# One block instead of two: the set-up of an attention and FFN kernel ordered among the first batch's work, with its staging laid over late buffers

## The reference

```
x = x + attention(layernorm(x), ctx, ctx)      # q = xn @ Wq.T + bq, k, v from ctx; q and k rotated by a phase per head
x = x + ffn(layernorm(x))
ffn: gf = sigmoid(MLP of the mean over the 1024 rows)
     out = x;  3 times: tf = sigmoid(gelu(gelu(gelu(out@w1)@w2)@w3)@w4)
                        out = out + (0.1 + range * (0.7*gf + 0.3*tf - 0.5) * 2) * twist(out)
```

## Time and profile before

| | us |
|---|---|
| median of 3 runs | 1504.09 |
| lowest and highest | 1503.36, 1508.3 |
| profiled execution, its own time | 1504.29 |
| its span, first to last instruction | 1502.2 |

### The profile page before, as it was taken

One profiled execution on the slowest core, in us unless ns is written; L12 is line 12 of the kernel. 1 busy time (PEld: TensorE's weight loads), 2 busy tenths in 40 slices (PEclk: granted clock), 3 DMA queues, 4 the chain that ended last, 5 costly groups with the idle time before them and its releaser, 6 DMA issues.

```text
span 1502.2 us, 29586 instructions
## 1 busy us (share of the span) xinstructions
PE 1322.3 (88%) x11288; PEld 930.1 (62%) x11288; DVE 1144.5 (76%) x2247; ACT 1058.3 (70%) x1949; POOL 643.8 (43%) x499
## 2 busy tenths in 40 slices
PE   6556789898999899999999899989999899989765
PEld 3333376666766586657766676658666676658553
DVE  3749538996599958996799759995898759983476
ACT  2635258876698769877797678877787768876565
POOL 0304114563255615563355516561455426561463
PEclk9866899999999999999999999999999999999986
DMA  8203400321124031312124122403132113301001
GB/s 271 85 11 70 110 2 18 65 57 50 51 57 75 1 106 34 60 39 65 43 57 75 32 75 44 78 12 96 26 64 54 50 57 57 71 1 43 1 15 43
DMA packets 156399, 83.36 MB, mean 55 GB/s; under 512 B 138978, under 2 KB 140770, under 8 KB 154211
## 3 DMA queue, kind: packets, MB, share of 16 engines
q1 hardware_dynamic: 156258, 81.47, 22.5%
HBM read 27.97 MB, written 19.92 MB: 32 GB/s over the span
## 4 chain that ended last, share of the span: by engine, by line
PE 54%; DVE 21%; ACT 9%; issue 6%; POOL 4%; DMA 1%; ACTq 0%; DVEq 0%
PE ps L283 20%; PE ps L241 9%; PE ps L298 8%; PE ps L196 7%; DVE prob L1666 2%; DVE mx L1658 2%; PE ps L318 2%; DVE pr L1688 2%; DVE z L1759 2%; PE ps L173 2%; POOL Y L2732 2%; DVE h L1738 2%; POOL h L2716 2%; DVE sm L1673 1%; PE ps L214 1%
## 5 line engine op out<-in xcount | busy, mean ns | idle before, releaser
L2716 POOL TENSOR_TENSOR h<-z,h 128x512 f16<-128x512 f32 x192 | 250.1, 1311 | 363.7 <-DVE h L1731 363.7
L283 PE MATMUL ps<-x2T,W 128*128 128x256 f16 x3072 | 356.6, 274 | 7.3 <-ACT Y L774 4.6
L283 PEld LDWEIGHTS ps<-x2T,W 128*128 128x128 f16 x3072 | 298.9, 98 | 53.6 <-issue 8.4
L298 PE MATMUL ps<-h,W 128*128 128x256 f16 x2304 | 283.6, 280 | 25.2 <-POOL h L2716 25.1
L298 PEld LDWEIGHTS ps<-h,W 128*128 128x128 f16 x2304 | 226.8, 100 | 74.5 <-issue 36.8
L2709 POOL TENSOR_TENSOR prob<-prob,rc 128x512 f32<-128x512 f32 x128 | 149.7, 1190 | 95.6 <-DVE rc L1682 95.5
L241 PE MATMUL ps<-WO,xoT 128*128 128x512 f16 x768 | 180.6, 386 | 4.4 <-DVE xoT L1693 4.4
L196 PE MATMUL ps<-xoT,WQ 128*128 128x512 f16 x768 | 175.2, 386 | 1.4 <-DVE xoT L1641 1.4
L787 ACT ACTIVATE z<-z,b_col 128x256 f32<-128x256 f32 x256 | 115.6, 499 | 33.1 <-DVE z L1759 32.8
L241 PEld LDWEIGHTS ps<-WO,xoT 128*128 128x128 f16 x768 | 75.9, 99 | 92.2 <-DVE xoT L1693 6.5
L196 PEld LDWEIGHTS ps<-xoT,WQ 128*128 128x128 f16 x768 | 76.0, 99 | 89.3 <-issue 5.9
(11 more groups left out here) (148 smaller groups left out, 2373.9 us busy)
## 6 DMA issues: line engine op xcount, KB each, us to landing
xin<-x SPq DMA_DIRECT2D x16, 1024.0 KB, 6.3
out<-ot SPq DMA_DIRECT2D x64, 256.0 KB, 3.4
kv_blocks<-kv SPq DMA_DIRECT2D x8, 384.0 KB, 3.8
kvb<-kv_blocks SPq DMA_DIRECT2D x8, 384.0 KB, 3.1
pT<-pr SPq DMA_TRANSPOSE x128, 3.2
ctx_s<-ctxT SPq DMA_DIRECT2D x4, 256.0 KB, 3.5
wv_s<-wvT SPq DMA_DIRECT2D x1, 1024.0 KB
wk_s<-wk SPq DMA_DIRECT2D x1, 1024.0 KB, 9.6
```

Source lines behind the costliest of these rows:

```text
L283: mm = e.matmul(ps[:, BANK_F + L, at * LBLK:(at + 1) * LBLK], w, v, start=(n == 0), stop=(n == 3 * C - 1))
L298: mm = e.matmul(ps[:, BANK_F + L, m * LBLK:(m + 1) * LBLK], w, v, start=(c + m + a == 0), stop=(c == C - 1 and m == C2 - 1 and a == 2))
L2716: e.tensor_tensor(h1[:, L, LO, pair(n)], z[:, L, pair(n)], h1[:, L, HI, pair(n)], ALU.subtract).then_inc(lg[L]["lo1"], 1)
```

## The change

There is now one block. The function `setup` is gone; its work is cut into pieces (`wq_turn`, `wk_turn`, `bias`, `kmul`, `vmul` on TensorE; `wq_hi`, `wk_out`, `k_hi`, `v_hi`, `w_hi` on ScalarE; `wq_lo`, `bias_out`, `k_lo`, `v_lo`, `w_lo`, `w_neg` and others on VectorE), and they stand in the lists of the batches, among the first steps of batch 0. Wq and x come first in the loads. K's low parts are all VectorE's. The four memsets of `kv` on VectorE come later. V uses three PSUM banks in turn and so waits for `v_lo` of three batches before. K and V of batch 0 go from `kv` to `kvb` directly, within SBUF; those of the others still go through DRAM, each with a semaphore of its own. The staging tiles are allocated ahead of x2T, pT, pr, Y, z and the FFN's other buffers and given free before them, so they share memory; the first steps that write there wait for the pieces that read the staging. The lists of the batches were written anew and differ from before by small moves; instructions and tiles of the batches are the same.

```diff
+            def vmul(bt):
+                if bt < 3:
+                    e.wait_ge(su["k_out"], bt + 2)
+                else:
+                    e.wait_ge(su["v_lo"], 2 * (bt - 3) + 2)
...
             def y(p, k, h, m):
...
+                    if u == 0:
+                        for n in range(1, B):
+                            e.wait_ge(kv_stored[n], 16)
+                        e.wait_ge(su["w_lo"], 6)
...
+            def k_lo(m):
+                for h in range(HPC):
+                    rows = slice(DK * h, DK * h + DK)
+                    e.wait_ge(su["k_hi"], HPC * m + h + 1)
+                    e.tensor_tensor(kpart(LO)[rows, :, m, h % 2], k32[rows, m], kpart(HI)[rows, :, m, h % 2],
+                                    ALU.subtract).then_inc(su["k_lo"], 1)
...
-            t1(0, 0, 0); t1(0, 0, 1); t1(0, 0, 2); t1(0, 0, 3)
+            wq_turn(0, 0); wq_turn(0, 1); wq_turn(0, 2); wq_turn(0, 3)
+            wk_turn(0, 0); wk_turn(0, 1); wk_turn(0, 2); wk_turn(0, 3)
+            bias(0)
+            kmul(0, 0); kmul(0, 1); kmul(0, 2); kmul(0, 3)
+            vmul(0, 0)
+            t1(0, 0, 0)
+            vmul(0, 1); vmul(0, 2); vmul(0, 3)
+            t1(0, 0, 1)
...
-            def kv(b):
+            def kv_load(b):
                 if b:
                     e.wait_ge(sg["s"], 8 * b)
                     e.wait_ge(sg["pv"], 4 * b)
-                e.dma_start(kvb[:].rearrange("p a n -> p (a n)"), kv_dram[b]).then_inc(sg["kv_loaded"], 16)
+                    e.wait_ge(kv_stored[b], 16)
+                    src = kv_dram[b]
+                else:
+                    e.wait_ge(su["v_hi"], 2)
+                    e.wait_ge(su["v_lo"], 2)
+                    e.wait_ge(su["k_lo"], HPC * C)
+                    src = kv[:, 0].rearrange("p a n -> p (a n)")
+                e.dma_start(kvb[:].rearrange("p a n -> p (a n)"), src).then_inc(sg["kv_loaded"], 16)
...
+            load("wq", wq_s[:], by_chunk(wq))
+            load_x(0)
+            load("wk", wk_s[:], by_chunk(wk))
...
+            load_x(1)
+            load("wo", wo_s[:], by_chunk(woT))
...
+            kv_load(0)
+            kv_store(0, 1); kv_store(0, 2); kv_store(0, 5); kv_store(0, 3); kv_store(0, 4); kv_store(0, 6); kv_store(0, 7)
```

More of the change, by code:

```diff
@@ L36 @@
 KV = KCOLS + PAIRS * DK
+ATT_PAD = 577
 def passes(parts_a, parts_b):
@@ L140, in program @@
             "alpha", "t_out", "out")}
+        su = {n: sem(n) for n in (
+            "consts", "zero_v", "zero_g", "angle", "sines", "rotation", "v_mul", "v_hi", "v_lo", "bias_mul", "bias_out", "bo_split",
+            "wk_mul", "wk_out", "k_mul", "k_out", "k_hi", "k_lo", "w_hi", "w_lo", "w_neg", "last_row", "wq_mul",
+            "wq_hi", "wq_lo", "scalars")}
+        loaded = {n: sem(f"in_{n}") for n in (
+            "phases", "turns", "ctx", "wv", "wk", "bqk", "wq", "wo", "bo", "w1", "w2", "w3", "last", "g1", "g2", "scal", "cols")}
         stored = [sem(f"stored{i}") for i in range(OUTS)]
@@ L896, in scalar_program @@
             yc(0, 0, 1, 2)
+            qh(1, 0, 0)
             act2(0, 0, 0, 0, 0)
-            qh(1, 0, 0)
+            xn1(1, 1, 0)
+            qh(1, 0, 1)
             act2(0, 0, 0, 0, 1)
@@ L1374, in scalar_program @@
             hi2(6, 0, 0, 0)
+            xn1(7, 1, 2)
             qh(7, 0, 2)
@@ new lines, in k_lo, with v_lo @@
+            @first
+            def k_lo(m):
+                for h in range(HPC):
+                    rows = slice(DK * h, DK * h + DK)
+                    e.wait_ge(su["k_hi"], HPC * m + h + 1)
+                    e.tensor_tensor(kpart(LO)[rows, :, m, h % 2], k32[rows, m], kpart(HI)[rows, :, m, h % 2],
+                                    ALU.subtract).then_inc(su["k_lo"], 1)
+            @first
+            def v_lo(bt):
+                for h in range(2):
+                    rows = slice(KEYS * h, KEYS * h + KEYS)
+                    src = ps[rows, BANK_V[bt % 3], 0:D2].rearrange("p (r n) -> p r n", r=PAIRS)
+                    e.wait_ge(su["v_hi"], 2 * bt + h + 1)
+                    e.tensor_tensor(vpart(LO)[rows, bt], src, vpart(HI)[rows, bt], ALU.subtract).then_inc(su["v_lo"], 1)
@@ new lines, in w_lo, with w_neg @@
+            @first
+            def w_lo(n):
+                e.wait_ge(su["w_hi"], n + 1)
+                dst, src = split_parts[n]
+                e.scalar_tensor_tensor(dst[:, LO], src[:], WSCALE, dst[:, HI], ALU.mult, ALU.subtract).then_inc(su["w_lo"], 1)
+            @first
+            def w_neg():
+                e.wait_ge(su["w_lo"], 2)
+                for p in (HI, LO):
+                    e.tensor_scalar(W1[:, p, C:C + 2], W1[:, p, 1:3], -1.0, None, ALU.mult).then_inc(su["w_neg"], 1)
@@ new lines, in sync_program @@
+            load("bqk", b_s[:, 1], bk)
+            load("wv", wv_s[:], by_chunk(wvT))
+            load("wv", bv_s[:], row(bv))
+            load_x(1)
+            load("wo", wo_s[:], by_chunk(woT))
+            load("bo", bo_s[:], row(bo).partition_broadcast(P))
+            load("last", last_s[:, 0:1], cw4)
+            load("last", last_s[:, 1:2], gw3)
+            for n, a in enumerate((arange, cb4, gb3)):
+                load("scal", scal_s[:, n:n + 1], row(a).partition_broadcast(P))
+            load("w1", w1_s[:], by_chunk(cw1))
```

1210 lines of the change are left out of this document (609 added, 601 removed).

## The result

| | before | after |
|---|---|---|
| time, median of 4 runs each (lowest to highest) | 1504.41 us (1503.36 to 1508.30) | 1465.75 us (1464.11 to 1466.76) |
| span of the profiled execution | 1502.2 us | 1464.2 us |
| first scores of batch 0 | 104.56 | 79.24 |
| from there to the first scores of batch 1 | 132.2 | 135.0 |
| six stretches, batch 1 to batch 7 | 995.2 | 983.9 |

In the profiled executions the first scores come 25.3 us earlier (forecast 22.4), the first stretch gives 2.8 back, and the rest, forecast as nothing, is 11.3 + 4.3 = 15.6 us shorter.

What follows compares the result with a forecast made beforehand. The prediction saw a serial set-up of small steps delaying batch 0's first scores to 104.56 us; scores 22.4 us earlier, less 0.5 in batch 0's softmax, took 1504.3 to 1482.4, said as 1482.5 us, range 1474.5 to 1491.5.

Steps and rivals of the forecast that it cites:

- Step 1: Set-up loads: Wq lands at 9 us, x block 0 at 12.3, Wo at 26.5, 6 us later than before.
- Rival A: Set-up: a stall on ScalarE or VectorE, as from Wo landing at 35, eats half the gain; 1493 us, chance 0.09.
- Steps 2 and 3: Set-up products: Wk at half clock, bias product done at 26.8 us; K 14.00 us plus 3 for a half-clock start.
- Bounds: Low: full clock for Wk and K (4.5 us), batches slightly shorter, 1475 us; high: late Wo, slower low parts, 1491.
- Step 4: VectorE in the set-up: K's 16 low parts at 0.68 us each, other weights' low parts, first xl1 at 57.4 us.
- Step 5: V pieces alternate with x's transposes on TensorE; the first Q product starts at 68.7 us, before at 90.03.
- Step 6: First Q product to scores: Q 10.4 us at full clock, V 7 2.45, transposes 0.65; scores at 82.2 us.
- Sum: Whole kernel: scores 22.4 us earlier, less 0.5, changed order in the batches taken as nothing; 1482.4, said as 1482.5 us.
- rival D: Batches: the new order gives besides, xn1(p,1,0) filling ScalarE's 1.2 us wait, 1 us or more each; 1474 us, chance 0.11.
- The cost I did charge, 0.5 us: Batch 0's softmax: v_hi(7) and v_lo(7) now stand inside it, 0.84 us, half in a hole, so 0.5.
- Rival B: Set-up: TensorE stays at half clock throughout, scores at 108.7 us, no gain; 1508 us, chance 0.03.
- Rival C: Batches: new order costs more than the start gives, l2 ahead of tile 2's scores on TensorE; 1517 us, chance 0.05.

Runs made afterwards that it cites:

- e11: Changed kernel with half of K's 16 low parts given back from VectorE to GpSimd; 1466.49 us.
- e2: Kernel before, its two blocks and layout kept, with every engine's list from batch 1 on in the changed kernel's order; 1491.12 us.
- e1: Changed kernel with every engine's list from batch 1 on in the order of before, set-up and batch 0 kept; 1479.22 us.
- e7: Changed kernel with only ScalarE's list from batch 1 on in the order of before; 1468.76 us.
- e14: Kernel before with only GpSimd's product mulg(p,1,0,2) put behind both am steps in batches 1 to 6; 1500.27 us.
- e8: Changed kernel with only TensorE's list from batch 1 on in the order of before; 1471.40 us.
- e6: Changed kernel with only VectorE's list from batch 1 on in the order of before; 1477.46 us.
- e10: Changed kernel with VectorE's xl2(b,0,0) put back behind the second pair of statistics in batches 2 to 6; 1466.18 us.
- e13: Changed kernel with GpSimd's product mulg(p,1,0,2) put ahead of both am steps in all eight batches; 1477.12 us.

## Why the prediction was wrong in size and right in kind

The sign, the mechanism of the start and the order of the terms held; the range did not. By its own steps:

- **Step 1 (loads)**: Wo landed at 24.8 instead of 26.5. Rival A's late load did not come, yet ScalarE waited 1.0 us for it, since it was through with xn at 23.8 instead of 28.
- **Steps 2 and 3 (Wq, Wk, K)**: too slow by 5 us at the end of the bias product (22.0 instead of 26.8), and K took 13.98 us instead of 17. VectorE reached wq_lo at 16.7 instead of 18.6. For the rest I had charged half clock for the pause; TensorE ran Wk's last 24 matmuls in 2.94 us and K at a full clock. This was the gain named in "Bounds", low. (The list of K's ends also gives the last piece 1 us more than the two ahead of it, for which no row stands.)
- **Step 4 (VectorE, which carries most)**: right. 16 low parts at 0.68 and G's at 1.22 + 0.42; the first low part of x at 51.1 instead of 57.4, since all began earlier. e11 confirms why 0.68 was the number to take: beside GpSimd the median is 1.53.
- **Step 5**: from there to Q, 14.6 us instead of 11.3. Here the clock did fall (0.72 and 0.64), and of the V pieces two took 3.03 and 3.67 us. The half clock I had put at K came at V. Q at 65.7, forecast 68.7.
- **Step 6**: right; 13.5 us from Q to scores, as forecast. First scores 79.24 instead of 82.2.
- **Sum, the failing step**: "The changed order in the batches I take as nothing." It gives 14.1 and 13.5 us in e2 and e1. It is rival D, mis-sized (0 in the sum, 8 us in the rival, about 13 measured) and under-weighted (0.11), and its reason was wrong: what I named for it, ScalarE's xn1(p,1,0), belongs to the list that e7 prices at 3.0 us for all its moves. The largest single move found is GpSimd's mulg(p,1,0,2): 6.4 us in e14. The view that would have led there was open: the row of c <- c in the kernel before, shown above, has instances of 293 and of 1242 ns, and GpSimd's product runs beside the long one (664.62 to 666.13 beside 665.03 to 666.27). I had used this very effect in step 4 and did not look for it in the batches.
- **The cost I did charge, 0.5 us** for v_hi(7) and v_lo(7) in batch 0's softmax: the first stretch was 2.8 us longer. The first stretch's length also moves between kernels with the same lists up to there (133.2 to 135.3 us), so at least 1 us of it is real and the rest is not settled.
- **Rival B** fell with K's full clock. One of its readings was off: before, the granted clock over 95 to 98 us is 1.00 already, so it was back within 5 us of the Q product's start at 90.03, and not only behind 8 us of it. **Rival C**: the scores of tile 2 came 1.3 us later in the stretch (554.38 - 542.05 = 12.33 instead of 11.02), but the product of the first probabilities 0.2 us earlier (615.76 - 542.05 = 73.71 instead of 644.61 - 570.67 = 73.94), so the delay is absorbed within the batch. e8, with TensorE's old list, takes 5.6 us more: that engine's moves gain and don't cost. TensorE in the changed kernel:

```profile
554.38 0.84 PE L301 MATMUL ps<-kvb,qT 64*128 64x128 f16 x24
...
615.76 0.84 PE L317 MATMUL ps<-pT,kvb 64*32 64x512 f16 x24
```


The start by itself was forecast at 21.9 us and measured at 26.0 (before to e1) and 25.4 (e2 to after): 3.5 to 4 us too little, and e1's 1479.2 lies inside the range. Step by step the errors went both ways (K 8 us earlier in all, Q only 3), so that the first scores came within 3.0 us of the forecast is in part luck. What put the time outside is the order.

What stays open: how the 13.5 us divide among the moves. One engine's old list costs 11.7, 5.6 or 3.0 us, GpSimd's one move some 6 to 8, which is more than 13.5 together; the moves overlap and the sum over engines means nothing. Which of VectorE's moves is behind e6's 11.7 us is not known: its c <- c is short in five of the six middle stretches, and the one move tried, in e10, is worth nothing. Why the first scores of kernels with one and the same set-up come anywhere from 77.4 to 81.2 us isn't settled either.

## What to carry to other kernels

A change in the order of a tuned schedule is not nothing because it is small: look for each line whose longest instance is several times its shortest, find who ran beside the long one, and count that difference once per repetition; then expect the clock to add to it at times: a delay of under 1 us went together here, in one middle stretch, with 2 us more at a lower clock, and in the last 40 us of e13 with 3.4 more. When a start is brought forward, ask which engine is full right behind it: what is deferred must go into that engine's waits, not past the first scores. And a list swapped for one engine alone doesn't give that engine's share; test the single suspected move in both kernels, in the same batches of each.

## What the runs showed of the hardware that was not expected

- A VectorE operation on one operand in SBUF (c <- c, 128x256 in float32) also stretches from 0.29 to 1.24 us beside a GpSimd product of 128x512; it ended 0.16 us behind it. I had looked for this only in operations on two operands.
- Eight 32x512 low parts beside GpSimd's take 1.53 us in the median, 0.68 alone.
- TensorE held its full clock over K (13.98 us) behind a pause of 2.5 us, Wk's last 24 matmuls (2.94) and 16 of one column (1.84), but had 0.72 and 0.64 among V pieces and transposes with waits of 1.5 to 2.0 us between.
- In the last stretch, where TensorE is busy for 81% of the time, kernels with equal matmuls differ by up to 11 us of TensorE's busy time there (216.7 us in after and e2, 228.2 in e14) at mean clocks from 0.94 down to 0.90.
